# Cross-attention scores in 32 x 64 tiles instead of 64 x 128, with four PSUM banks shared by two chunks

## The reference

```
y_dca = y[:, -DCA:, :]           # the last 16 tokens of the context
y_main = y[:, :-DCA, :]          # the other 1585
q = _ln((x @ Wq + bq).reshape(b, s1, H, HD), qn_w, qn_b)      # H = 16 heads of HD = 32
kv = concat([y_main @ Wk + bk, y_main @ Wv + bv]).reshape(b, s2, H, 2 * HD)
k = _ln(kv[..., :HD], kn_w, kn_b)
v = kv[..., HD:]
ctx = softmax(q k^T * HD ** -0.5) v          # per head, all in float32
ctx_dca = the same with the keys and values of y_dca
return (ctx + ctx_dca) @ Wo + bo
```

## Time and profile before

| | |
|---|---|
| median of three runs | 1407.89 us |
| profiled execution | 1407.75 us, span 1405.9 us |
| TensorE busy (matmul) | 1314.5 us, 93% |
| VectorE busy | 990.8 us, 70% |
| ScalarE busy | 850.2 us, 60% |
| GpSimd busy | 311.7 us, 22% |
| mean granted TensorE clock | 0.976 |

### The profile page before, as it was taken

The page is one execution under the profiler, slowest core; times in us unless marked ns, Lnnn a source line. Parts: engine busy times, 40 slices in busy tenths (PEclk is TensorE's granted clock), DMA queues, the critical chain, the costliest instruction groups (busy, mean ns, idle before and its releaser), DMA issues. The chain is left out here.

```text
span 1405.9 us, 42510 instructions
## 1 busy us (share of the span) xinstructions
PE 1314.5 (93%) x16104; PEld 1078.5 (77%) x16104; DVE 990.8 (70%) x1811; ACT 850.2 (60%) x1535; POOL 311.7 (22%) x354
## 2 busy tenths in 40 slices
PE   6889999999999999999999999999999799965896
PEld 3468888888888888888888888888877677744785
DVE  7847677776767776776767777776867656665764
ACT  2346776766777676767766767667666333334653
POOL 2312121221212121221212121221211302111465
PEclk9989999999999999999999999999999999986999
DMA  7042110210210120111112110210200100016887
GB/s 267 16 163 75 47 33 17 96 33 17 70 53 24 32 96 17 33 47 66 33 32 78 36 33 17 97 33 17 75 21 2 65 1 32 31 47 211 210 189 136
DMA packets 35098, 91.26 MB, mean 65 GB/s; under 512 B 4039, under 2 KB 7626, under 8 KB 33418
## 3 DMA queue, kind: packets, MB, share of 16 engines
q1 hardware_dynamic: 28064, 72.38, 15.5%
q0 software_dynamic: 6432, 16.32, 5.2%
q10 hardware_dynamic: 434, 0.08, 0.0%
HBM read 71.93 MB, written 36.01 MB: 77 GB/s over the span
## 5 line engine op out<-in xcount | busy, mean ns | idle before, releaser
L1105 POOL TENSOR_TENSOR y_lo<-y_sb,y_hi 128x256 fp32r<-128x256 f32 x190 | 143.1, 753 | 803.1 <-ACT y_hi L984 803.1
L1018 ACT ACTIVATE ksq<-kc 128x512 f32<-128x512 f32 x200 | 126.4, 632 | 230.0 <-DVE kc L1142 226.4
L1142 DVE TENSOR_TENSOR kc<-psum,bk_sb 128x512 f32<-128x512 f32 x200 | 137.6, 688 | 142.4 <-PE psum L106 139.8
L1035 ACT ACTIVATE probs<-psum 128x1024 f32<-128x1024 f32 x208 | 201.0, 1023 | 39.0 <-PE psum L1327 37.7
L1327 PE MATMUL psum<-qbd,k 64*128 64x128 f32 x3328 | 211.9, 278 | 0.1
L1327 PEld LDWEIGHTS psum<-qbd,k 64*128 64x128 f32 x3328 | 193.3, 188 | 14.0 <-issue 6.3
L1197 DVE TENSOR_TENSOR total<-total,probs 128x1024 f32<-128x1024 f32 x160 | 194.1, 1213 | 1.4 <-ACT probs L1035 1.2
L106 PE MATMUL psum<-wk_hi,y_hi 128*128 128x512 f32 x400 | 177.3, 443 | 11.5 <-issue 8.3
L1148 DVE TENSOR_REDUCE kss<-ksq 128x16 f32<-128x512 f32 x200 | 134.1, 670 | 46.2 <-ACT ksq L1018 45.9
L106 PE MATMUL psum<-wv_hi,y_hi 128*128 128x512 f32 x400 | 157.5, 394 | 2.4 <-ACT v_sb L1011 2.4
L997 ACT ACTIVATE k<-psum,cols_sb 128x512 f32<-128x512 f32 x192 | 150.7, 785 | 13.9 <-PE psum L87 13.9
(11 more groups left out here) (272 smaller groups left out, 2033.5 us busy)
## 6 DMA issues: line engine op xcount, KB each, us to landing
y_sb<-in_y SPq DMA_DIRECT2D x48, 512.0 KB, 3.6
slots_dram<-in_blank SPq DMA_DIRECT2D x9, 2080.0 KB
expert_raw<-in_experts SPq DMA_DIRECT2D x8, 1024.0 KB, 6.8
x_sb<-slots_dram SPq DMA_DIRECT2D x23, 260.0 KB, 3.1
x_sb<-in_x SPq DMA_DIRECT2D x1, 1536.0 KB, 10.2
wq<-in_wq SPq DMA_DIRECT2D x4, 256.0 KB, 4.3
xa_wo<-in_wo SPq DMA_DIRECT2D x1, 1024.0 KB, 12.1
y_tail<-in_y_tail SPq DMA_DIRECT2D x8, 128.0 KB, 22.0
```

The lines of the kernel that those rows point to most:

```text
L1018: nc.scalar.activation(sq[:, buf(n)], kc[:, buf(n)], ACT.Square).then_inc(s["ksq"], 1)
L1035: nc.scalar.activation(probs[:, buf(u), :], psum[:, bank:bank + 2, :].rearrange("p a n -> p (a n)"), ACT.Exp, scale=SCALE).then_inc(s["ex" ...
L1105: nc.gpsimd.tensor_tensor(g.y_lo[:, buf(n)], src, g.y_hi[:, buf(n)].bitcast(F32), ALU.subtract).then_inc(s["ylo"], 1)
L1142: nc.vector.tensor_tensor(kc[:, buf(n)], psum[:, K_BANK, :], g.bk[:], ALU.add).then_inc(s["kb"], 1)
```

## The change

For full chunks, `scores` becomes `chunk_scores`: 32 matmuls instead of 8. Each takes the 32 rows of one head, 64 of the chunk's keys as weight columns (so the output stands on partitions 0 to 63 or 64 to 127), and that head's own 64 queries from `qbd`, none of the zeros. The four row strips r write to four banks, 3 to 6. A chunk fills 256 columns in each of them: the first chunk of a group the left halves of the four banks, the second chunk the right halves. So the exponential of the first chunk now waits for the scores of the second too (`sc` of u + 1), and the scores of a group wait, once at its start, for both exponentials of the group before. The exponential reads four pieces of 256 columns, and `place` and `heads_in` follow the new order of heads in `probs`. The tail's scores are as before (`tail_scores`), in banks 1 and 2.

```diff
-    S_PLACES = (S_BANK, S_BANK + 2, V_BANK)
+    TAIL_BANK = V_BANK
...
-        def place(h):
-            return (h // 2 % 2) * 8 + h // 4 * 2 + h % 2
+        def place(h, u):
+            return (h // 2 % 2) * 8 + h // 4 * 2 + h % 2 if tail(u) else h % 4 * GROUPS + h // 4
...
                 def exps(i, u, j):
-                    act.wait_ge(s["sc"], unit(i, u))
+                    act.wait_ge(s["sc"], unit(i, u + 1 if j == 0 else u))
                     act.wait_ge(s["pv"], unit(i, last_unit(u)))
                     if not tail(u):
                         act.wait_ge(s["pa"], added(i, last_unit(u)))
-                    bank = S_PLACES[j]
-                    nc.scalar.activation(probs[:, buf(u), :], psum[:, bank:bank + 2, :].rearrange("p a n -> p (a n)"),
-                                         ACT.Exp, scale=SCALE).then_inc(s["ex"], 1)
+                    if tail(u):
+                        out, scored = probs[:, buf(u), :], psum[:, TAIL_BANK:TAIL_BANK + 2, :].rearrange("p a n -> p (a n)")
+                    else:
+                        out = probs[:, buf(u), :].rearrange("p (r n) -> p r n", r=4)
+                        scored = psum[:, S_BANK:S_BANK + 4, j * GROUPS * SQ:(j + 1) * GROUPS * SQ]
+                    nc.scalar.activation(out, scored, ACT.Exp, scale=SCALE).then_inc(s["ex"], 1)
...
+                def chunk_scores(u, j, guarded):
+                    at_n = [slice(j * GROUPS * SQ + n * SQ, j * GROUPS * SQ + (n + 1) * SQ) for n in range(GROUPS)]
...
+                    for n in range(GROUPS):
+                        for half in range(2):
+                            keys = slice(half * SQ, (half + 1) * SQ)
+                            for r in range(4):
+                                rows, cols = blocks[r]
+                                last = pe.matmul(psum[keys, S_BANK + r, at_n[n]], k32[rows, k_buf(u), n, keys],
+                                                 g.qbd[rows, n, cols], start=not guarded, stop=True, skip_group_check=True)
+                    return last
...
                     pe.wait_ge(s["ke"], projected(i, proj_of(u)))
-                    if j < 2:
-                        pe.wait_ge(s["ex"], unit(i, u - 3 if column(u) < 2 else u - 2))
-                    else:
+                    if j == 0:
+                        pe.wait_ge(s["ex"], unit(i, u - 2 if column(u) == 0 else u - 1))
+                    if j == 2:
                         pe.wait_ge(s["ve"], values_done)
                         pe.wait_ge(s["ke"], turned_done)
...
+                    last = tail_scores(u, guarded) if tail(u) else chunk_scores(u, j, guarded)
                     last.then_inc(s["sc"], 1)
```

More of the change, by code:

```diff
@@ L882, in by_rows, with heads_in @@
             return ap.rearrange("p (g j q) -> p g j q", g=2, j=2)
-        def heads_in(ap, r):
-            return ap.rearrange("p (a g b n) -> p a g b n", a=2, g=2, b=2)[:, r % 2, :, r // 2, :]
+        def heads_in(ap, r, in_tail):
+            if in_tail:
+                return ap.rearrange("p (a g b n) -> p a g b n", a=2, g=2, b=2)[:, r % 2, :, r // 2, :]
+            return ap.rearrange("p (a j g b q) -> p a b g j q", a=2, j=2, g=2, b=2)[:, r % 2, r // 2]
         def normalise(b, wait, engine):
@@ L1298, in turn, with tail_scores @@
                     transposes(pe, psum[:, TR_BANK, :], kn[:, buf(n), :], g.ident[:]).then_inc(s["tr"], 1)
+                def chunk_scores(u, j, guarded):
+                    at_n = [slice(j * GROUPS * SQ + n * SQ, j * GROUPS * SQ + (n + 1) * SQ) for n in range(GROUPS)]
+                    if guarded:
+                        for r in range(4):
+                            pe.matmul(psum[:, S_BANK + r, at_n[0].start:at_n[-1].stop], select[:, 0, :],
+                                      shift[:].rearrange("s (n r q) -> s n r q", n=GROUPS, r=4)[:, :, r, :],
+                                      start=True, stop=False, skip_group_check=True)
+                    for n in range(GROUPS):
+                        for half in range(2):
+                            keys = slice(half * SQ, (half + 1) * SQ)
+                            for r in range(4):
+                                rows, cols = blocks[r]
+                                last = pe.matmul(psum[keys, S_BANK + r, at_n[n]], k32[rows, k_buf(u), n, keys],
+                                                 g.qbd[rows, n, cols], start=not guarded, stop=True, skip_group_check=True)
+                    return last
+                def tail_scores(u, guarded):
+                    out = [[psum[:, TAIL_BANK + a, n * P:(n + 1) * P] for a in range(2)] for n in range(GROUPS)]
+                    if guarded:
+                        for n in range(GROUPS):
+                            for a in range(2):
+                                pe.matmul(out[n][a], select[:, {TAIL: 1, UNITS - 1: 2}[u], :],
+                                          shift[:, (2 * n + a) * P:(2 * n + a + 1) * P],
+                                          start=(n == 0), stop=False, skip_group_check=True)
+                    for n in range(GROUPS):
+                        for a in range(2):
+                            rows = slice(a * 2 * HD, (a + 1) * 2 * HD)
+                            last = pe.matmul(out[n][a], k32[rows, k_buf(u), n, :], g.qbd[rows, n, :],
+                                             start=not guarded, stop=True, skip_group_check=True)
+                    return last
                 def scores(i, u, j, guarded, values_done=None, turned_done=None):
@@ L1345, in weighted @@
                                 last = pe.matmul(psum[r * HD:(r + 1) * HD, bank, k * SQ:(k + 1) * SQ], v,
-                                                 probs[:, buf(u), place(h) * SQ:(place(h) + 1) * SQ],
+                                                 probs[:, buf(u), place(h, u) * SQ:(place(h, u) + 1) * SQ],
                                                  start=(k == 0 and (column(u) == 0 or n == 1)), stop=tail(u), skip_group_check=True)
@@ L1349, in weighted, with counts @@
                         for n, bank in ((1, V_BANK), (0, O_BANK)):
-                            last = counts(bank, g.counted[:, half * 2 + n], probs[:, buf(u), :], n == 1)
+                            last = counts(bank, g.counted[:, half * 2 + n], probs[:, buf(u), :], n == 1, True)
                         pe.wait_ge(s["pa"], added(i, u - 1))
-                        last = counts(O_BANK, g.counted[:, 4], total[:], True)
+                        last = counts(O_BANK, g.counted[:, 4], total[:], True, False)
                     last.then_inc(s["pv"], 1)
-                def counts(bank, rows, src, stop):
+                def counts(bank, rows, src, stop, in_tail):
                     for r in range(4):
-                        last = pe.matmul(psum[r * HD:(r + 1) * HD, bank, KD * SQ:2 * KD * SQ], rows, heads_in(src, r),
+                        last = pe.matmul(psum[r * HD:(r + 1) * HD, bank, KD * SQ:2 * KD * SQ], rows, heads_in(src, r, in_tail),
                                          start=False, stop=stop, skip_group_check=True)
```

## The result

The changed kernel takes 1473.8 us (median of 4 runs, 1471.1 to 1477.8), the kernel before in the same comparison 1407.8 us: ratio 1.046, 95% interval 1.044 to 1.048. It is 4.6% slower; the forecast was 3.5% faster.

The account below looks back on a forecast made before the run. TensorE was taken to bound cross-attention. Shorter scores would save 85 us, some 35 lost to VectorE's norms and the exponentials, leaving 49.5: 1407.75 - 49.5 = 1358 us; own range 1335 to 1375, 8 in 10 from 1335 to 1412.

Parts of the forecast that it names:

- Which engine bounds it: In cross-attention, TensorE is busy 932 of 943 us and sets the end; VectorE, at 73%, is the one to watch.
- That eight tiles overlap: In the score matmuls, four row strips by two column halves run at once, though no row shows more than four tiles.
- That a record then costs 7 ns: In the score run, 128 records at 7 ns take 0.90 us, plus 0.19, so 1.09 us a group.
- The term saved per group: Scores on TensorE fall from 1.98 to 1.09 us a group: 0.89 saved, 85 us over 96 groups.
- rival 1: Score tiles overlap only somewhat beyond four: 10 ns a record, 1.47 us a run, 1382 us in all; chance 0.18.
- That the shared wait costs nothing: First exponential on ScalarE, waiting for both chunks' scores, still starts 1.3 us after the scores' start: no added cost.
- That instructions are fetched ahead: TensorE's longer instruction stream costs nothing if fetched ahead; 77 more packets would cost 92 us if each were waited for.
- Rival 3: Grown instruction stream cancels the gain, up to 1450 us; chance 0.09 including mixtures within 0.5%, a third of it slower.
- The waits for VectorE: TensorE, arriving early, waits for key-bank emptying or norms; with the exponentials this loses some 35 of 85 us.
- rival 2: Only four score tiles at once: run stays 1.99 us, exponentials start later, +13 us, 1421; chance 0.15.

Follow-up runs that it names:

- the kernel with half of the heads: Changed kernel with the scores of only 8 of the 16 heads, 64 matmuls and 64 loads a group, same tiles, banks and waits: 1357.1 us, 0.963.

## Why the prediction was wrong

**Which engine bounds it** was right: TensorE stays last everywhere, and its idle time went straight into the end.

**That eight tiles overlap** was right, and the forecast's way to see it too (four of a quad in 20 ns): eight begin in 0.05 us. **That a record then costs 7 ns** failed. It held for some rounds of the first 32 records; over the run it is 10.4 ns, and the 256 instructions take 1.52 us (1.42 if they move 32 columns instead of 64). The run was taken at 1.09 us. The term saved per group is 0.46 us, not 0.89: 44 us of the 85. That is rival 1's pace (10 ns a record, a run of 1.47 us). The prediction had the figure in hand: rival 1 noted that 3.5 ns an instruction is twice the pace of the weighted sums, the fastest that any row showed, and gave it 0.18. A pace that no row shows should have been an end of the range and not the value taken.

**That the shared wait costs nothing** hung on that 7 ns. Alone it costs 12 us, at the place and nearly the price given to it (the values behind a tail, 13 us); within the changed kernel 3.5 us of waiting are left of it.

**That instructions are fetched ahead** was the step that turned the sign. Rival 3 counted the packets right (77, they were 71), and its 92 us if each were waited for is of the size of what came. It was given 0.09 on one piece of evidence: the 256 records of the earlier trace rows run without a gap. But those stand behind slow work; the change puts 256 more of them behind the 128 of the weighted sums, and a fetch needs 2.2 to 2.9 us from its start to the first new instruction. 384 take some 2.55 us (1.03 and 1.52). That 92 us is near the measured 73 is luck: rival 3 had every packet wait 1.2 us, and what happened were 56 gaps of 1.2 us each, at ends of blocks inside or behind a burst. The question was not how many bytes come in a millisecond but how many instructions start in 2.5 us. The Trainium skill ("Runtime: NRT & Kernel Launch", Instruction fetch mechanics) calls the crossing of a 16 KB block "mostly hidden" since instructions are dispatched more slowly than they are filled; the trace agrees with it for the kernel before, with 0.1 us of idle time ahead of its scores, and not for the changed one, with 54.2 us.

**The clock** stands nowhere in the prediction, which took 1.00 from the kernel before. The gaps brought stretches at 0.50, and the projections lost 10 us by them.

**The sum as it is**, by the two profiled executions (1471.3 against 1405.9 us of span, +65), each part of TensorE's time counted from start to start. The full chunks' scores would take 96 x 0.46 = 44 us less, and missing instructions put 96 x (2.28 - 1.52) = 73 us on top, 28 in sum; the runs' own totals (218.6 for 191.7) give +26.9. Tails' scores take 25.7 us against 14.3 (17.7 in the kernel with half of the heads, where few instructions are missing: 3.4 for a second change of the tiles' form, 8 for gaps): +11.4. Keys and values take 583.5 against 565.6: +17.9, of it 10 from the clock, 3.5 from waits for exponentials, some 4 from missing instructions and 1 from VectorE. Turns, weighted sums and counts take 3.6 us more, cross-attention's scores start 2.7 us later, and what lies behind it takes 2.9 us more. 26.9 + 11.4 + 17.9 + 3.6 + 2.7 + 2.9 = 65.4.

**The waits for VectorE**, group by group, were hardly tested, since TensorE never came early enough; where it did (half of the heads) they appeared in turns and keys, together 27 us. Of the rivals none was the result; rival 1's pace with rival 3's missing instructions is, and of rival 2's later exponentials 3.5 us.

## What to carry to other kernels

Smaller tiles trade array time for instructions. Before cutting a matmul into more pieces, count how many instructions (weight loads too, and the passes of an f32 product) will stand together, neighbours included, and divide by the fastest pace that a row shows; if more than about one fetch of 256 starts within the 2.5 us that a fetch takes here, idle time comes that no semaphore shows, as "issue" inside a run of equal instructions. To tell such gaps from others, number the engine's records: here they all stand at the same remainder by 256. And an order that breaks the burst isn't free: moving work on one engine moves what is queued behind its evacuation on another; here that cost 56 us where 54 were to be won. Hold each new order against the old form in the same order: only so do the tiles (0.46 us a group) and the order (-0.22) come apart.

## What the runs showed that I had not expected

- The first 64 instructions of a run start at 4 to 5 ns each, later ones at 5 to 6 ns, nearly independent of the moving columns (32 or 64): 32 matmuls in 0.29 us, the next 31 in 0.37.
- Instructions stand ready for a short burst only: 384 together lose 54 us of idle time in 96 groups, 256 together 8 to 11, 128 together 3 to 4, at the same 206 packets (158 for the 8.1 us of half of the heads). The gaps stand at ends of blocks of 256 instructions, 55 of 56 in the changed kernel.
- Behind eight of the gaps, each of 1.8 to 2.4 us, the granted clock was 0.50 for 27 us in all; a projection matmul takes 0.43 us there instead of 0.23.
- A tile of 32 rows by 128 columns with 64 moving columns starts four records in 0.11 us, one of 32 by 64 eight in 0.06: most likely the load's columns count where they are more than the moving ones.
